# Linear attention and a recurrent block on one Trainium2 core: the last tile's context, the key bias and the last residuals change place

## The chip, the cores and the metric

The kernel runs on one core of a Trainium2 chip. The metric is the device time of one execution in microseconds (us), the median of several. PE is TensorE, DVE is VectorE, ACT is ScalarE, POOL is GpSimd, SP is SyncE (it issues the DMAs here). Each engine executes its own list of instructions in order; what another engine must have done first is a wait on a semaphore that stands in that list, and everything behind a waiting instruction waits too.

## The reference, cut to what matters

The input x is (8, 512, 128) in fp32. A linear attention with a residual and a layer norm is followed by a gated recurrence that scans the first axis, so 8 steps of 512 rows, and a second residual and layer norm.

```python
Q = elu(x @ Wq.T + bq) + 1;  K = elu(x @ Wk.T + bk) + 1;  V = x @ Wv.T + bv
KV = einsum('bnd,bne->bde', K, V)
Z = einsum('bnd,bd->bn', Q, K.sum(axis=1) + 1e-06)
x = layernorm(x + (einsum('bnd,bde->bne', Q, KV) / Z[..., None]) @ Wo.T + bo)
def step(c, xt):                       # over x[0], x[1], ... x[7]
    ft = sigmoid(xt @ wf.T + c @ uf.T + bf);  it = sigmoid(xt @ wi.T + c @ ui.T + bi)
    gt = tanh(xt @ wc.T + c @ uc.T + bc)
    return ft * c + it * gt
h = tanh(x @ wo.T + c_final @ uo.T + bo)
x = layernorm(x + h)
```

## The kernel before, in words

**Tiles.** A tile is one of the 8 slices of x, 512 rows by 128 features, held as four chunks of 128 rows (C = 4, H = 2 is half of them). D is 128. All of it is loaded at the start, tile by tile, once by rows (`x_rows`) and once transposed (`x_cols`).

**Attention of a tile.** PE forms the keys in the bank `ps_k`: four products of x_cols and Wk (L374), each of them fp32 and two instructions in the trace, and then one matmul of `ones_r` with the row of the key bias plus one (L378), all of one accumulation group. ACT takes the exponential (`key_exp`, L664), and DVE combines it with ps_k to elu + 1 (`key_max`, L878, semaphore k_ok). `queries` (L384), `query_exp` (L669, L670) and `query_sum` (L929) do the same for the queries. `keys_x` (L393) multiplies the keys with x, ACT copies that (`xk_copy`, L713), and `key_values` on PE (L403, L404), with the sums of the keys that POOL forms (`key_sums`, L283, L288), gives key-values already multiplied with Wo; DVE adds a constant (`key_values`, L937, semaphore kvo_ok). These small products lie in the bank of `ps_ctx` in the columns behind the context, and for tile 7 in `ps_k` (function `small`, L198). `context` (L415) multiplies the queries with them: 2 x 2 blocks of 129 columns, the last of which is Z, in the two banks of `ps_ctx`. DVE takes 1/Z (`reciprocal_z`, L861), and `residual` (L867) adds x, one chunk at a time; its semaphores y_ok and y_small_ok say that the two banks of the context are free. `attention_end` is residual, `statistics` (L841) and `variance` (L847).

**First layer norm.** POOL raises variance + eps to the power -1/2 (`reciprocal_root`, L292); DVE normalises chunks (L856). For tiles 0, 6 and 7 (SHARED_LN) ACT does two of the four chunks (`first_normalise`, L708), for which POOL first makes a shift (L297). PE turns the tile (`x1_turned`, L429) into `ps_x1`, from which ACT takes a rounded high part (`x1_high`, L717), DVE the rest (`x1_low`, L873) and ACT a whole copy (`x1_whole`, L721).

**Recurrence.** The three gates stand in the banks ps_f, ps_i and ps_c. `gates_x` (L443 to L452) adds the products of x1 in split precision, `gate_s` (L470 to L475) those of the state, high part and low part; they need `state_high` on ACT (L688) and `state_low` on POOL (L316), in two late steps on DVE (L914). `gates_tanh` on ACT (L678) is three tanhs: forget, input, candidate. DVE forms `kept_state` (L889), `new_state` (L896) and `next_state` (L903), together `step`. The list STEPS (L47) orders the steps: 0 to 3 are tiles 0 to 3 in full width; after that each tile is stepped in two halves, the lower halves of tiles 4 to 7 being steps 4, 5, 7 and 8, the upper ones 6, 9, 10 and 11.

**The order.** The first FULL_PERIODS periods (L239) are generated: in period n every engine does its share of the keys and queries of tile n + 1, the key-values and context of tile n, the first layer norm of tile n - 1 and the recurrence of tile n - 2. After them the order of every engine is written out by hand (POOL from L345, PE from L618, ACT from L760, DVE from L983). In it keys_x, key_values and context of tile 7 stand around the gates of step 5 on PE.

**Output.** UNITS (L52) divides the output into nine units of tiles and halves: units 0 to 3 are the lower halves of two tiles each, 4 to 6 the upper halves of two tiles, 7 and 8 the upper halves of tile 6 and of tile 7. Each has a bank (`unit_bank`, L159). PE forms the product with wo (`out_x`, L506), and adds what all tiles share, the final state's product, either directly (`out_s`, L522, units 0 and 4) or from a rounded copy in two parts g_hi and g_lo (`out_g`, `add_g`, L547, L551). ACT takes the tanh in place in the bank (`out_tanh`, L697, h_ok), DVE adds it to x1 (`second_residual`, L1010, w_ok), then `second_statistics` (L1018) and `second_variance` (L1026, L1028). POOL makes the root and the shift (L303, L310). The blocks of a unit are normalised by DVE (the first DVE_NORM[u], L1034) and ACT (the others, L702), and SP stores the unit when both have done (L265). In the last loops DVE does, for units 5 to 8, residual, statistics, variance of the unit and its share of normalise of the unit before; ACT does the tanh of unit u and its share of normalise of unit u - 2.

## Time and profile before

| | us |
|---|---|
| median of 3 runs | 105.56 (105.0 to 105.93) |
| the profiled execution, its own time | 106.08 |
| its span, first to last instruction | 104.3 |
| PE busy | 92.1 (88%) |
| DVE busy | 81.4 (78%) |
| ACT busy | 66.3 (64%) |
| POOL busy | 43.0 (41%) |

The granted clock of TensorE is 0.974 of full speed on the mean. All numbers of the trace are in us from the span's start. A line such as L374 is a line of the kernel before. In rows of a timeline the bracket at the end is how long the engine was idle before the instruction, and what ended that. A busy PE is modelled: matmuls overlap, and the duration shown is longer than the distance to the next one; the chain shows the distance.

### The profile page before, as it was taken

The numbers are of one execution on the slowest core, as the hardware profiler recorded it, in microseconds if no ns is written. First come the engines' busy times: TensorE is split into PE (matmuls) and PEld (weight loads), VectorE is DVE, ScalarE is ACT, GpSimd is POOL, SyncE is SP. The second block draws the span as 40 slices with busy tenths as digits, with TensorE's granted clock in tenths as the row PEclk, the third lists the DMA queues.
The fourth block names the chain that finished last, engine by engine and source line by source line (L and its number), as shares of the span: only waits on it lengthen the run. The fifth ranks groups of instructions, "written<-read, shape, count | busy, mean of one in ns | idle before, by whom it ended". The sixth has DMA issues, their size and how long they took to land.

```text
span 104.3 us, 1923 instructions
## 1 busy us (share of the span) xinstructions
PE 92.1 (88%) x611; PEld 79.7 (76%) x611; DVE 81.4 (78%) x236; ACT 66.3 (64%) x137; POOL 43.0 (41%) x64
## 2 busy tenths in 40 slices
PE   6998999999799999999999999998999999986000
PEld 4778779689388968978888989988899998965000
DVE  3136398979999995898689997986356999999960
ACT  1327579476485594576659565759465859777651
POOL 2006268328448048019206622650500238266660
PEclk9999999999999999999999999999999999999955
DMA  2869996000000000000000000000000000443362
GB/s 40 287 214 409 384 387 236 0 0 3 0 0 0 0 0 0 9 0 0 0 0 0 0 6 0 0 3 3 6 0 0 0 0 6 158 137 108 105 209 89
DMA packets 5269, 7.30 MB, mean 70 GB/s; under 512 B 491, under 2 KB 3084, under 8 KB 5260
## 3 DMA queue, kind: packets, MB, share of 16 engines
q1 hardware_dynamic: 4828, 6.85, 18.7%
q10 hardware_dynamic: 432, 0.33, 1.2%
q8 instruction: 5, 0.08, 0.4%
q14 instruction: 4, 0.03, 0.1%
HBM read 5.08 MB, written 2.10 MB: 69 GB/s over the span
## 4 chain that ended last, share of the span: by engine, by line
PE 54%; DVE 32%; issue 4%; ACT 4%; POOL 2%; POOLq 0%; DVEq 0%; ACTq 0%
PE ps_k L374 7%; PE ps_ctx L393 6%; DVE stats L1018 6%; PE ps_q L384 6%; DVE x L1010 5%; PE ps_ctx L415 4%; PE ps_f L363 4%; DVE x L856 4%; DVE s L903 2%; DVE x L1034 2%; DVE new L896 2%; PE ps_x L429 2%; PE ps_f L452 2%; PE ps_k L378 2%; PE ps_ctx L403 2%
## 5 line engine op out<-in xcount | busy, mean ns | idle before, releaser
L316 POOL TENSOR_TENSOR s_lo<-s,s_hi 128x512 fp32r<-128x512 f32 (+1 forms) x8 | 8.1, 1016 | 22.7 <-ACT s_hi L688 22.7
L303 POOL TENSOR_TENSOR rstd<-var_eps,minus_half 128x4 f32<-128x4 f32 (+1 forms) x9 | 9.3, 1034 | 13.8 <-DVE var_eps L1026 13.8
L292 POOL TENSOR_TENSOR rstd<-var_eps,minus_half 128x4 f32<-128x4 f32 x8 | 9.0, 1122 | 9.3 <-DVE var_eps L847 9.0
L702 ACT ACTIVATE x<-x,shift,rstd 128x128 f32<-128x128 f32 x20 | 8.6, 488 | 3.0 <-POOL shift L310 2.8
L283 POOL TENSOR_TENSOR k_pair<-k_rows 128x256 f32<-128x256 f32 x8 | 6.3, 784 | 9.8 <-DVE k_rows L878 9.8
L856 DVE TENSOR_SCALAR x<-x,stats,rstd 128x128 f32<-128x128 f32 x26 | 9.9, 439 | 0.3 <-POOL rstd L292 0.3
L664 ACT ACTIVATE k_exp<-ps_k,minus_one 128x512 f32<-128x512 f32 x8 | 5.5, 686 | 6.2 <-PE ps_k L378 6.2
L374 PE MATMUL ps_k<-wkq,x_cols 128*128 128x128 f32 x64 | 9.3, 294 | 0.0
L867 DVE SCALAR_TENSOR_TENSOR x<-ps_ctx,z_inv,x_rows 128x128 f32<-128x128 f32 x32 | 9.1, 343 | 0.1
L374 PEld LDWEIGHTS ps_k<-wkq,x_cols 128*128 128x128 f32 x64 | 8.6, 209 | 0.4 <-DMA wkq<-w_kq 0.4
L717 ACT ACTIVATE x_hi<-ps_x 128x512 fp32r<-128x512 f32 x8 | 4.8, 597 | 6.5 <-PE ps_x L429 6.5
L415 PEld LDWEIGHTS ps_ctx<-kvo,q_cols 128*128 128x128 f32 x64 | 8.2, 191 | 0.8 <-issue 0.5
L678 ACT ACTIVATE th_f<-ps_f,half_b 128x256 f32<-128x256 f32 (+1 forms) x11 | 5.8, 529 | 4.7 <-PE ps_f L475 4.4
L415 PE MATMUL ps_ctx<-kvo,q_cols 128*128 128x129 f32 x64 | 8.5, 276 | 0.0
L384 PE MATMUL ps_q<-x_cols,wkq 128*128 128x512 f32 x16 | 8.2, 592 | 0.0
L393 PEld LDWEIGHTS ps_ctx<-k_rows,x_rows 128*128 128x128 f32 x56 | 7.1, 191 | 1.0 <-issue 0.7
L393 PE MATMUL ps_ctx<-k_rows,x_rows 128*128 128x128 f32 x56 | 7.5, 277 | 0.4 <-DVE k_rows L878 0.4
L688 ACT ACTIVATE s_hi<-s 128x256 fp32r<-128x256 f32 (+1 forms) x10 | 4.9, 499 | 4.2 <-DVE s L903 4.2
L889 DVE SCALAR_TENSOR_TENSOR keep<-th_f,s 128x256 f32<-128x256 f32 (+1 forms) x11 | 5.4, 491 | 2.7 <-ACT th_f L678 2.7
L896 DVE SCALAR_TENSOR_TENSOR new<-th_i,th_c 128x256 f32<-128x256 f32 (+1 forms) x12 | 6.1, 509 | 1.7 <-ACT th_c L678 1.7
L678 ACT ACTIVATE th_i<-ps_i,half_b 128x256 f32<-128x256 f32 (+1 forms) x11 | 5.8, 527 | 2.0 <-PE ps_i L475 2.0
L903 DVE SCALAR_TENSOR_TENSOR s<-keep,new 128x256 f32<-128x256 f32 (+1 forms) x12 | 6.2, 515 | 0.8
(176 smaller groups left out, 283.3 us busy)
## 6 DMA issues: line engine op xcount, KB each, us to landing
x_cols<-xt SPq DMA_DIRECT2D x8, 256.0 KB, 7.0
x_rows<-x SPq DMA_DIRECT2D x8, 256.0 KB, 7.0
out<-x SPq DMA_DIRECT2D x7, 256.0 KB, 2.2
wgate<-w_gate SPq DMA_DIRECT2D x1, 384.0 KB, 6.9
out<-x SPq DMA_DIRECT2D x2, 128.0 KB, 1.8
wkq<-w_kq ACTq DMA_DIRECT2D x1, 131.0 KB, 3.7
wvo_in<-w_vo_in ACTq DMA_DIRECT2D x1, 128.0 KB, 3.7
wout<-w_out SPq DMA_DIRECT2D x1, 128.0 KB, 6.5
```

Of the source, the lines that this page charges most:

```text
L292: nc.gpsimd.tensor_tensor(rstd[:, b], var_eps[:, b], minus_half[:], ALU.pow).then_inc(rstd_ok, 1)
L303: nc.gpsimd.tensor_tensor(part_of(rstd, u, T), part_of(var_eps, u, T), minus_half[:, 0:nt * H].rearrange("p (t c) -> p t c", c=H), ALU.pow ...
L374: nc.tensor.matmul(ps_k[:, c * D:(c + 1) * D], x_cols[:, a, c], wkq[:, WK_T * D:(WK_T + 1) * D], start=(c == 0), stop=False, skip_group_ch ...
L384: nc.tensor.matmul(ps_q[:], wkq[:, WQ_T * D:(WQ_T + 1) * D], x_cols[:, a].rearrange("p c d -> p (c d)"), start=True, stop=True).then_inc(q ...
L393: mm = nc.tensor.matmul(small(a)[:, 0:D], x_rows[:, a, c], k_rows[:, a % 2, c], start=(c == 0), stop=(c == C - 1))
L415: mm = nc.tensor.matmul(ctx_view[:, c // 2, c % 2], q_cols[:, b % 2, c], kvo[:, b % 2], start=True, stop=True, skip_group_check=True)
L678: nc.scalar.activation(out_tile[:, part], ps[:, part], ACT.Tanh, bias=bias, scale=scale).then_inc(ok, 1)
L702: nc.scalar.activation(x1[:, t, c], x1[:, t, c], ACT.Identity, bias=shift[:, t, c:c + 1], scale=rstd[:, T + t, c:c + 1]).then_inc(y2_act_o ...
L856: nc.vector.tensor_scalar(x1[:, b, c], x1[:, b, c], mean_of(b, c), rstd[:, b, c:c + 1], ALU.subtract, ALU.mult).then_inc(x1_ok, 1)
L867: ins = nc.vector.scalar_tensor_tensor(x1[:, b, c], ctx_view[:, c // 2, c % 2, 0:D], z_inv[:, b % 2, c:c + 1], x_rows[:, b, c, 0:D], ALU.m ...
L896: nc.vector.scalar_tensor_tensor(new[:, part], th_i[:, part], 1.0, th_c[:, part], ALU.add, ALU.mult).then_inc(new_ok, 1)
L903: nc.vector.scalar_tensor_tensor(state(t)[:, part], keep[:, part], 0.5, new[:, part], ALU.mult, ALU.add).then_inc(s_ok, 1)
```

## The change

1. *Key bias.* For tiles 4 to 7 ACT writes the key bias plus one into `ps_k` (a new function `key_bias`, placed between the forget tanh and the input tanh of the period before), and the four key products accumulate on it, so that the bias matmul is not issued. The bias is loaded once more, to all 128 partitions (64 KB, SP's queue, behind wgate), and POOL adds one to it after `halve_weights`.
2. *Tile 7.* The generated periods are six; the seventh is written out together with what followed. In it keys_x, key_values and context of tile 7 follow those of tile 6, before the gates of step 5. The context of tile 7 lies in banks of its own, ps_k (behind the small products) and ps_q, so that it waits for no residual of tile 6. DVE does the residual of tile 7 ahead of step 5 and its statistics behind it; ACT and POOL follow that order. On ACT the xk copy of tile 7 stands between the forget tanh and the input tanh of step 4. The banks of the units change accordingly: units 0 and 1 take those of ps_ctx, units 2 and 3 ps_k and ps_q.
3. *Last units.* For units 6, 7 and 8 PE adds x1 onto the tanh in PSUM, with the identity as the stationary operand (`add_x1`); DVE's residual is left out, and the statistics and the normalise read the sum from PSUM. DVE_NORM of units 5 to 8 goes from 1, 2, 1, 1 to 2, 0, 2, 2.

The diff, cut to its core:

```diff
          (7, 0, H), (5, H, C), (6, H, C), (7, H, C)]
-FULL_PERIODS = 7
+FULL_PERIODS = 6
 UNITS = [(0, 2, 0), (2, 2, 0), (4, 2, 0), (6, 2, 0), (0, 2, H), (2, 2, H), (4, 2, H), (6, 1, H), (7, 1, H)]
-DVE_NORM = [1, 1, 1, 2, 2, 1, 2, 1, 1]
+DVE_NORM = [1, 1, 1, 2, 2, 2, 0, 2, 2]
+IN_PSUM = (6, 7, 8)
 SHARED_LN = (0, 6, 7)
+BIAS_BY_PE = 4
...
         ctx_view = ps_ctx[:, :, 0:2 * DZ].rearrange("p b (c d) -> p b c d", d=DZ)
-        g_bank = [ps_x1[:, 0:H * D], ps_q[:, 0:H * D]]
-        unit_bank = [ps_k[:], ps_q[:], ps_ctx[:, 0, :], ps_ctx[:, 1, :], ps_x1[:], ps_k[:], ps_ctx[:, 0, :],
-                     ps_ctx[:, 1, :], ps_f[:]]
+        g_bank = [ps_x1[:, 0:H * D], ps_ctx[:, 1, 0:H * D]]
+        unit_bank = [ps_ctx[:, 0, :], ps_ctx[:, 1, :], ps_k[:], ps_q[:], ps_x1[:], ps_ctx[:, 0, :], ps_k[:], ps_q[:],
+                     ps_f[:]]
         kq_in, vo_in, gate_in, out_in = sem("kq_in"), sem("vo_in"), sem("gate_in"), sem("out_in")
-        row_in, batt_in = sem("row_in"), sem("batt_in")
+        row_in, batt_in, bk_in = sem("row_in"), sem("batt_in"), sem("bk_in")
...
                     sp.dma_start(wgate[:], w_gate).then_inc(gate_in, 16)
+                    sp.dma_start(bk_wide[:], rows[BK_ROW].partition_broadcast(D)).then_inc(bk_in, 16)
...
                                         ALU.mult).then_inc(shift1_ok, 1)
+            def key_bias():
+                pool.wait_ge(bk_in, 16)
+                nc.gpsimd.tensor_scalar(bk_wide[:], bk_wide[:], 1.0, None, ALU.add).then_inc(bk_ok, 1)
...
                     halve_weights()
+                    key_bias()
...
                     split_state_low()
+            state_low(3)
+            reciprocal_root(5)
+            key_sums(7)
...
                     pe.wait_ge(k_ok, a)
+                if a >= BIAS_BY_PE:
+                    pe.wait_ge(k_bias_ok, a - BIAS_BY_PE + 1)
                 for c in range(C):
-                    nc.tensor.matmul(ps_k[:, c * D:(c + 1) * D], x_cols[:, a, c], wkq[:, WK_T * D:(WK_T + 1) * D],
-                                     start=(c == 0), stop=False, skip_group_check=True)
+                    mm = nc.tensor.matmul(ps_k[:, c * D:(c + 1) * D], x_cols[:, a, c], wkq[:, WK_T * D:(WK_T + 1) * D],
+                                          start=(c == 0 and a < BIAS_BY_PE), stop=(a >= BIAS_BY_PE),
+                                          skip_group_check=True)
+                if a >= BIAS_BY_PE:
+                    mm.then_inc(k_mm, 1)
+                    return
...
                 pe.wait_ge(kvo_ok, b + 1)
-                if b >= 1:
+                if 1 <= b < T - 1:
                     pe.wait_ge(y_ok, b)
-                if b == T - 1:
-                    pe.wait_ge(y_small_ok, b)
                 for c in range(C):
-                    mm = nc.tensor.matmul(ctx_view[:, c // 2, c % 2], q_cols[:, b % 2, c], kvo[:, b % 2],
+                    mm = nc.tensor.matmul(ctx_of(b, c // 2)[:, c % 2], q_cols[:, b % 2, c], kvo[:, b % 2],
...
                     pe.wait_ge(out_in, 16)
-                    pe.wait_ge(kvo_ok, T)
+                    pe.wait_ge(y_ok, T - 1)
                 if u == 1:
-                    pe.wait_ge(q_relu_ok, T)
+                    pe.wait_ge(y_small_ok, T - 1)
...
                                  start=False, stop=True, skip_group_check=True).then_inc(out_mm, 1)
+            def add_x1(u):
+                t0, nt, c0 = UNITS[u]
+                ps = unit_bank[u]
+                pe.wait_ge(h_ok, u + 1)
+                for j in range(nt):
+                    mm = nc.tensor.matmul(ps[:, j * H * D:(j + 1) * H * D], ident[:],
+                                          x1[:, t0 + j, c0:c0 + H].rearrange("p c d -> p (c d)"),
+                                          start=False, stop=True, skip_group_check=True)
+                mm.then_inc(psum_w_mm, 1)
...
                     x1_turned(b)
+            keys(7)
+            queries(7)
+            gates_x(4)
+            keys_x(6)
+            gate_s(0, 4)
+            key_values(6)
             keys_x(7)
+            gate_s(1, 4)
+            gate_s(2, 4)
+            context(6)
+            key_values(7)
+            x1_turned(5)
+            context(7)
             gates_x(5)
-            key_values(7)
             gates_s(5)
-            context(7)
...
                 add_g(u)
+                if u - 1 in IN_PSUM:
+                    add_x1(u - 1)
+            add_x1(len(UNITS) - 1)
...
                 nc.scalar.activation(out_tile[:, part], ps[:, part], ACT.Tanh, bias=bias, scale=scale).then_inc(ok, 1)
-            def gates_tanh(k):
+            def forget_tanh(k):
                 tanh(ps_f, f_mm, k, keep_ok, th_f, 0.5, half_b[:, 0:1] if k else first_b[:, 0:1], f_ok)
+            def input_tanh(k):
...
                 tanh(ps_c, c_mm, k, new_ok, th_c, 1.0, col[:, BC:BC + 1] if k else first_b[:, 2:3], c_ok)
+            def gates_tanh(k):
+                forget_tanh(k)
+                input_tanh(k)
...
                 for t, c in blocks(u)[DVE_NORM[u]:]:
-                    nc.scalar.activation(x1[:, t, c], x1[:, t, c], ACT.Identity, bias=shift[:, t, c:c + 1],
-                                         scale=rstd[:, T + t, c:c + 1]).then_inc(y2_act_ok, 1)
+                    nc.scalar.activation(x1[:, t, c], sum_of(u)[:, t - UNITS[u][0], c - UNITS[u][2]], ACT.Identity,
+                                         bias=shift[:, t, c:c + 1], scale=rstd[:, T + t, c:c + 1]).then_inc(y2_act_ok, 1)
...
                                          scale=rstd[:, b, c:c + 1]).then_inc(x1_act_ok, 1)
+            def key_bias(a):
+                if a == BIAS_BY_PE:
+                    act.wait_ge(bk_ok, 1)
+                act.wait_ge(k_ok, a)
+                nc.scalar.activation(ps_k[:].rearrange("p (c d) -> p c d", d=D),
+                                     bk_wide[:].unsqueeze(1).to_broadcast([D, C, D]), ACT.Copy).then_inc(k_bias_ok, 1)
...
                 if t is not None:
-                    gates_tanh(t)
+                    forget_tanh(t)
+                    key_bias(k + 1)
+                    input_tanh(t)
...
                     x1_high(b)
+            key_exp(7)
+            state_high(3)
+            x1_whole(4)
+            query_exp(7)
+            xk_copy(6)
+            forget_tanh(4)
+            xk_copy(7)
+            input_tanh(4)
+            x1_high(5)
             state_high(4)
-            xk_copy(7)
...
             gates_tanh(5)
+            first_normalise(6)
             state_high(5)
-            first_normalise(6)
+            x1_high(6)
             gates_tanh(6)
-            x1_high(6)
...
                 dve.wait_ge(ctx_mm, b + 1)
-                nc.vector.reciprocal(z_inv[:, b % 2].rearrange("p (b c) -> p b c", c=2),
-                                     ctx_view[:, :, :, D]).then_inc(z_ok, 1)
+                if b < T - 1:
+                    nc.vector.reciprocal(z_inv[:, b % 2].rearrange("p (b c) -> p b c", c=2),
+                                         ctx_view[:, :, :, D]).then_inc(z_ok, 1)
+                    return
+                for half in range(2):
+                    nc.vector.reciprocal(z_inv[:, b % 2, half * H:half * H + H], ctx_of(b, half)[:, :, D]).then_inc(z_ok, 1)
             def residual(b, chunks, done):
-                dve.wait_ge(z_ok, b + 1)
+                dve.wait_ge(z_ok, b + 1 if b < T - 1 else T + 1)
                 for c in chunks:
-                    ins = nc.vector.scalar_tensor_tensor(x1[:, b, c], ctx_view[:, c // 2, c % 2, 0:D],
+                    ins = nc.vector.scalar_tensor_tensor(x1[:, b, c], ctx_of(b, c // 2)[:, c % 2, 0:D],
...
                     next_state(t)
-                if b >= 1 and a < FULL_PERIODS - 1:
+                if b >= 1:
                     x1_low(b)
+            attention_end(5)
+            key_max(7)
+            query_sum(7)
+            key_values(6)
+            normalise(5)
+            kept_state(4)
+            new_state(4)
+            reciprocal_z(6)
+            key_values(7)
+            next_state(4)
...
             dve.wait_ge(y_small_ok, 7)
-            key_values(7)
...
             variance(6)
+            reciprocal_z(7)
+            residual(7, range(H, C), y_small_ok)
+            residual(7, range(H), y_ok)
+            normalise(6)
             step(5)
-            normalise(6)
-            reciprocal_z(7)
-            attention_end(7)
-            kept_state(6)
+            dve.wait_ge(y_ok, 8)
+            dve.wait_ge(y_small_ok, 8)
+            statistics(7)
+            variance(7)
             x1_low(6)
+            step(6)
             normalise(7)
-            new_state(6)
-            next_state(6)
...
                 t0, nt, c0 = UNITS[u]
-                dve.wait_ge(w_ok, u + 1)
+                if u in IN_PSUM:
+                    dve.wait_ge(psum_w_mm, IN_PSUM.index(u) + 1)
+                else:
+                    dve.wait_ge(w_ok, u + 1)
...
                     st = nc.vector.bn_stats(stats[:, T + t, c0:c0 + H].rearrange("p c m -> p (c m)"),
-                                            x1[:, t, c0:c0 + H].rearrange("p c d -> p d c"))
+                                            sum_of(u)[:, t - t0].rearrange("p c d -> p d c"))
...
                 for t, c in blocks(u)[:DVE_NORM[u]]:
-                    nc.vector.tensor_scalar(x1[:, t, c], x1[:, t, c], mean_of(T + t, c), rstd[:, T + t, c:c + 1],
-                                            ALU.subtract, ALU.mult).then_inc(y2_ok, 1)
+                    nc.vector.tensor_scalar(x1[:, t, c], sum_of(u)[:, t - UNITS[u][0], c - UNITS[u][2]], mean_of(T + t, c),
+                                            rstd[:, T + t, c:c + 1], ALU.subtract, ALU.mult).then_inc(y2_ok, 1)
...
             for u in range(5, len(UNITS)):
-                second_residual(u)
+                if u not in IN_PSUM:
+                    second_residual(u)
...
```

In the part that is cut, `sum_of(u)` is the bank of the unit for units 6 to 8 and x1 for the others, and `ctx_of(b, half)` is ps_ctx for tiles 0 to 6, and for tile 7 `ps_k[:, DZ:3*DZ]` (half 0) and `ps_q[:, 0:2*DZ]` (half 1).

## Rows read from the trace of the kernel before

**Rows 1.** The page's first part: busy time, share, instructions.
```profile
PE 92.1 (88%) x611; PEld 79.7 (76%) x611; DVE 81.4 (78%) x236; ACT 66.3 (64%) x137; POOL 43.0 (41%) x64
```
**Rows 2.** Stages: length, PE, PEld, DVE, ACT, POOL busy; clock, DMA share, GB/s.
```profile
30.00:40.00 10.00, 10.00 (x63) 8.50 (x62) 9.85 (x27) 7.13 (x13) 5.24 (x6) 1.00 0.00 0
70.00:80.00 10.00, 9.64 (x76) 9.06 (x76) 5.75 (x14) 6.39 (x17) 1.72 (x3) 1.00 0.01 2
```
**Rows 3.** The chain that ended last, tile 6's keys: start, us, what.
```profile
44.21 0.89 PE ps_k L374 x8
45.10 0.23 PE ps_k L378
```
**Rows 4.** The same chain between units 5 and 7.
```profile
95.82 0.60 DVE x L1010
...
97.48 0.25 DVE x L1034
97.73 0.34 DVE x L1010
```
**Rows 5.** Timeline of PE at 27 us and of DVE at 50 us.
```profile
26.91 0.59 PE L429 MATMUL ps_x<-ident,x 128*128 128x128 f32 x2 [0.56 <-DVE x L856]
...
50.36 0.29 DVE L937 TENSOR_TENSOR kvo<-ps_ctx,eps_z 128x129 f32<-128x129 f32 x1 [1.19 <-PE ps_ctx L404]
```
**Rows 6.** Timeline of ACT, period of tiles 5 and 6.
```profile
45.96 0.62 ACT L688 ACTIVATE s_hi<-s 128x512 fp32r<-128x512 f32 x1
...
51.05 0.69 ACT L678 ACTIVATE th_i<-ps_i,half_b 128x512 f32<-128x512 f32 x1 [0.45 <-PE ps_i L475]
```
**Rows 7.** Timeline of POOL; then a DMA issue, the last number its landing.
```profile
15.54 1.48 POOL L292 TENSOR_TENSOR rstd<-var_eps,minus_half 128x4 f32<-128x4 f32 x1 [0.73 <-DVE var_eps L847]
...
26.73 0.54 POOL L330 TENSOR_SCALAR uo_half<-wout 128x128 f32<-128x128 f32 x1
...
wgate<-w_gate SPq DMA_DIRECT2D x1, 384.0 KB, 6.9
```
**Rows 8.** Timeline of ACT and PE around steps 4 and 8.
```profile
58.52 0.47 ACT L678 ACTIVATE th_i<-ps_i,half_b 128x256 f32<-128x256 f32 x1 [0.67 <-PE ps_i L475]
...
71.23 0.60 PE L429 MATMUL ps_x<-ident,x 128*128 128x128 f32 x4
```
**Rows 9.** Timeline of DVE, states 4 and 5, tile 7's norm; POOL's root of tile 7.
```profile
60.51 0.42 DVE L903 SCALAR_TENSOR_TENSOR s<-keep,new 128x256 f32<-128x256 f32 x1
...
65.41 0.42 DVE L903 SCALAR_TENSOR_TENSOR s<-keep,new 128x256 f32<-128x256 f32 x1
...
66.53 1.13 DVE L867 SCALAR_TENSOR_TENSOR x<-ps_ctx,z_inv,x_rows 128x128 f32<-128x128 f32 x4
67.69 0.77 DVE L841 BATCH_NORM_STATS2 stats<-x 128x6 f32<-128x256 f32 x2
...
73.33 0.69 DVE L873 TENSOR_TENSOR x_lo<-ps_x,x_hi 128x512 fp32r<-128x512 f32 x1
...
68.74 1.18 POOL L292 TENSOR_TENSOR rstd<-var_eps,minus_half 128x4 f32<-128x4 f32 x1 [1.64 <-DVE var_eps L847]
```
**Rows 10.** Timeline of ACT and POOL in the last ten us.
```profile
94.14 0.58 ACT L697 ACTIVATE ps_ctx<-ps_ctx 128x512 f32<-128x512 f32 x1
...
96.81 1.26 ACT L702 ACTIVATE x<-x,shift,rstd 128x128 f32<-128x128 f32 x3 [1.02 <-POOL shift L310]
...
101.64 0.49 ACT L702 ACTIVATE x<-x,shift,rstd 128x128 f32<-128x128 f32 x1 [1.17 <-POOL shift L310]
...
100.38 0.79 POOL L303 TENSOR_TENSOR rstd<-var_eps,minus_half 128x2 f32<-128x2 f32 x1 [0.43 <-DVE var_eps L1026]
```
**Rows 11.** Groups by line and form: busy us, mean ns of one.
```profile
L867 DVE SCALAR_TENSOR_TENSOR x<-ps_ctx,z_inv,x_rows 128x128 f32<-128x128 f32 x32 | 9.1, 343 | 0.1
...
L1018 DVE BATCH_NORM_STATS2 stats<-x 128x6 f32<-128x256 f32 x16 | 6.2, 424 | 0.2
...
L1034 DVE TENSOR_SCALAR x<-x,stats,rstd 128x128 f32<-128x128 f32 x12 | 3.8, 341 | 0.6 <-POOL rstd L303 0.6
```

More of the change, by code:

```diff
@@ L97, in build @@
         batt = sb("batt", [D, D])
+        bk_wide = sb("bk_wide", [D, D])
         ident = sb("ident", [D, D])
@@ L200, in small, with ctx_of @@
             return ps_k[:, 0:DZ] if a == T - 1 else ps_ctx[:, 1, 2 * DZ:3 * DZ]
+        def ctx_of(b, half):
+            if b < T - 1:
+                return ctx_view[:, half]
+            tile = ps_q[:, 0:2 * DZ] if half else ps_k[:, DZ:3 * DZ]
+            return tile.rearrange("p (c d) -> p c d", d=DZ)
         def dve_chunks(b):
@@ L243, in periods, with sum_of @@
                 yield n + 1, n, n - 1 if n >= 1 else None, n - 2 if n >= 2 else None
+        def sum_of(u):
+            nt = UNITS[u][1]
+            if u in IN_PSUM:
+                return unit_bank[u][:, 0:nt * H * D].rearrange("p (t c d) -> p t c d", c=H, d=D)
+            return part_of(x1, u)
         def act_norms(units):
```

4 lines of the change are left out of this document (added).

## The prediction, made before the changed kernel was run

> **What bounds the kernel now.** I read the page's shares first, then the stages, then the chain that ended last, then the engines one by one where the change acts. The shares name PE (92.1 us of 104.3) with DVE behind it (81.4) [rows 1]. An average hides the order, so the stages come next: from 30 to 40 us PE is busy for all of 10 us, from 70 to 80 us DVE for only 5.75 [rows 2]. So there are three regimes. In the periods the chain is PE alone, a tile's four key products (0.89 us) and the key bias (0.23) back to back [rows 3]. From 58 to 80 us the chain goes to and fro between layer norms and the recurrence. From 80 us it is DVE without a gap: residual, statistics, variance, normalise, unit after unit [rows 4].
>
> **Key bias by ScalarE.** Four bias matmuls (tiles 4 to 7) leave PE, 4 x 0.235 = 0.94 us [rows 3]. Tile 4's is worth nothing: right behind it PE waits 0.56 us for DVE's normalise of tile 1, which neither edit touches [rows 5]. The other three lie in the unbroken PE chain: 0.70 us. That holds if DVE and ACT keep up. DVE idles 1.19 us per period before the kvo addition, so a period shorter by 0.23 leaves it slack [rows 5]. ACT gets a 128x512 write per period; the nearest row is the copy s_hi of that shape, 0.62 us [rows 6]. It stands between the forget and the input tanh, where ACT idles 0.45 us waiting for PE [rows 6]. So the input tanh moves by about 0.1 us and the candidate tanh, which waits for PE itself, by nothing. Bounds: 0 if another engine takes over, 0.94 if tile 4's counts too; I take 0.70. The extra DMA (64 KB, issued after wgate) and POOL's addition of 1.0 (a 128x128 POOL tensor_scalar took 0.54 us) fit the gap on POOL before the first root, 0.73 us [rows 7]. If the DMA landed late, POOL's queue would hold the root of tile 0; wgate, the issue before it, took 6.9 us to land, and the addition would run from 14.8, the start of that gap [rows 7]. I cost it at 0, at most 0.5.
>
> **Tile 7's context one period up.** No work disappears; its order changes on four engines. I walked both orders by hand with the durations of the trace, entering 0.70 us early. What is queued behind each wait decides:
> - ACT now holds the input and candidate tanh of step 4 behind the xk copy of tile 7. Before, th_i(4) ran at 58.52 [rows 8]. Now key_values(6) frees PE at about 57.4, keys_x(7) (0.89) is read at 58.5, the copy (0.28) ends at 58.75, th_i starts at 58.85 and th_c ends at 59.7. On DVE next_state(4) also stands behind the kvo addition of tile 7, whose matmuls follow context(6): 60.5. State 4 starts at 60.75; before it was 60.51 [rows 9].
> - The first half of what follows keeps its lead: statistics(6) start at about 62.8. Residual(7) goes out at 64.05 against 66.53, 2.5 us sooner [rows 9].
> - But residual(7) (1.13 us), its two reciprocals (0.2) and normalise(6) (0.5) now stand ahead of step 5. State 5 starts at 66.5 against 65.41: 1.1 us later [rows 9]. Statistics(7) stand behind step 5: 66.9 against 67.69. POOL does s_lo(5) up to 68.2 and only then root(7), 1.18 us by its row, and its shift; ACT's share of normalise(7) starts at 69.85 and PE turns the tile at 70.75 against 71.23 [rows 8, 9]. x_lo(7) follows at 72.85 against 73.33 [rows 9].
> So of the 0.70 us about 0.5 arrives at the steps 8 to 11. From there to 93 us both kernels issue the same instructions with the same waits, on other banks whose last users are done by then; the 0.5 us goes through unchanged. The bounds of this part: +1.2 (the lead kept, and layer norm 7 no longer behind s_lo(5) on POOL, 0.5) and -1.1 (state 5's delay carried through). I take +0.5.
>
> **x1 added in PSUM.** DVE loses the residual of units 6, 7, 8: 0.60 + 0.34 + 0.34 = 1.28 us [rows 4]. Its share of normalise goes from 1, 2, 1, 1 to 2, 0, 2, 2 blocks for units 5 to 8, plus 0.26. In return each unit goes tanh, PE, DVE. By the row of four 128-column f32 products (0.89 us for 512 columns [rows 3]) the identity product costs 0.87 us for unit 6 and 0.43 for units 7 and 8. In the times of before: tanh(6) ends 94.72 [rows 10], the product is readable at 95.9, where DVE is free at 95.8 after normalise(4): 0.1 lost. Statistics(6) to 96.65, variance, normalise(5) with 2 blocks to 97.4; unit 7's sum was ready at 97.05, so statistics(7) run at 97.4. Unit 8 is late: ACT's normalise(5) waits for shift(5) and starts at 96.81 [rows 10], now 2 blocks to 97.6, tanh(8) to 97.95, product to 98.65, statistics to 99.1, variance to 99.3, by the chain of before (0.43 for one unit of 256 columns [rows 11]). POOL: root(6) 96.9 to 98.0, root(7) to 99.1, root(8) 99.35 to 100.15 (0.79 by its row [rows 10]). DVE normalises both blocks of unit 8 up to 100.8. Before, the chain ended with shift(8) and an ACT block at 101.64 + 0.49 = 102.13 [rows 10]. That is 1.3 us. The store of unit 8 now stands behind those of 6 and 7 in SP's queue and in the transfers: 0.1 back. Net 1.2.
> Not shown before are statistics, DVE and ACT normalises that read PSUM. DVE's residual, which reads a 128x128 block from PSUM, took 343 ns, the normalise from SBUF 341, statistics 424 [rows 11]: so 0 to 0.06 us for each of six instructions on the path, 0.1 taken, and ACT's four blocks are off the path.
> The Trainium skill speaks against this edit: "VectorE: DVE Perf Modes", section "Why PSUM operands drop a tier", says that an operand in PSUM caps fp32 at the single rate, where tensor_scalar from SBUF can have the double. By it the normalises of units 7 and 8 would take some 0.07 us more each, an estimate of 0.2 us on the path. The rows of SBUF and PSUM above are 2 ns apart, so the trace does not yet show the double rate being lost.
>
> **The sum.** Span 104.3 - 0.5 - 1.2 = 102.6. The profiled run took 106.08, 1.78 more than its span: 104.4. It stands 0.52 above the median of 105.56; taking that off gives **103.9 us**, 1.6% less. About 1% is what a measurement of this kernel tells from no change.
>
> **Rivals.**
> 1. *Only the tail gains (20%).* The restructured stretch eats the 0.70: th_i(4) 1.0 us behind its old place relative to the rest, and state 5 late, speak for it; that layer norm 7, not state 5, opened step 8 before, speaks against. 104.3 - 1.2 = 103.1 span, 104.4 on the median's scale.
> 2. *The tail is lost to hand-overs (12%).* The middle gives its 0.5, but tanh to PE to DVE costs as much as the residuals saved: if each of the three sums came 0.4 us after DVE is free, 1.2 us is gone. Against it: only unit 8's is late in my walk. 105.1.
> 3. *The middle gains more (13%).* DVE is idle for 4.25 of the 10 us from 70 to 80 [rows 2]; if the residual, 2.5 us sooner, lets layer norm 7 open step 8 by the whole lead of 0.70 and the 0.5 in which POOL holds its root, the exit lead is 1.2 and the time 103.2.
> 4. *Slower (7%).* The recurrence becomes the bound at step 5. The delays placed ahead of it add in full: tanh 0.94, reciprocals and residual(7) 1.33, normalise(6) 0.5, together 2.8; less 0.70 at entry it is 2.1 late, less 1.2 in the tail: 0.9 above before, 106.5. It decides once state 5 is written after about 68 us; my walk has 66.9, and steps 6 and 9, which do not need it, give cover.
> 5. *It does not do what it says (3%).* The bias by ACT comes after PE has reached the next keys, so that PE waits: tile 4's is ready at about 24.75 against 24.83, but there 0.56 us of slack follows; the later ones are written some 2 us before PE's next keys. With a wait of 0.4 us at each of three tiles it is 1.2 above the forecast, 105.1.
>
> **How the numbers follow.** My forecast has 45%, with its own range 103.3 to 104.5. Rivals 1, 3, 2, 5 and 4 reach from 103.2 to 106.5; leaving out 4 and part of 2, 5 and 3 gives 102.8 to 105.2. Faster by over 1% (below 104.5): the forecast nearly whole (0.43), rival 3 (0.13) and somewhat over half of rival 1 (0.12): 0.68. Slower by over 1% (above 106.6): half of rival 4 and what I overlooked, 0.07. The rest, 0.25, is within 1%.
>
> **What would show it.** Right: period length on PE 8.6 us instead of 8.83; ACT's bias write 0.6 us; state 5 later than before by about a microsecond while PE turns tile 7 about 0.5 earlier; no DVE residual for units 6 to 8, DVE waiting only for unit 8; the chain ending in POOL's root and a DVE normalise. Wrong: DVE waiting for PE at every one of the last three units; PE idle for over 1 us in all between 58 and 72 us; step 8's forget tanh starting later than 75.2 less 0.3.

## The result, and the profile after

The changed kernel took 103.94 us in the median of four executions (103.33 to 104.32), the kernel before 105.28 in the same comparison: ratio 0.9857, 95% interval 0.9815 to 0.9899. A later comparison of the same two gave 0.9843 (0.9799 to 0.9887). The forecast was 103.9 us. The profiled execution took 104.32 us with a span of 102.4, against 106.08 and 104.3. So the device time holds 1.92 us that lie outside the span, against 1.78 before.

The page's first part, of the changed kernel:
```profile
PE 93.8 (92%) x615; PEld 80.7 (79%) x615; DVE 80.6 (79%) x235; ACT 67.5 (66%) x140; POOL 42.7 (42%) x65
```
Its stages, columns as in [rows 2]:
```profile
30.00:40.00 10.00, 10.00 (x64) 8.56 (x63) 9.85 (x27) 7.56 (x14) 5.22 (x6) 1.00 0.00 0
70.00:80.00 10.00, 9.87 (x79) 9.31 (x78) 5.28 (x14) 6.52 (x17) 1.42 (x2) 1.00 0.01 2
```
The shares tell little: PE has more busy time than before (rows of matmuls overlap, and one that waits is drawn longer), and the gain lies in the order of work. What tells is the time between landmarks. I use five: the start of ACT's high part of tile 1 (A, 27.53 us before), PE's query product of tile 7 (B), the forget tanh of step 8 (C), DVE's statistics of unit 5 (D), the end of the last compute instruction (E), and the span's end (F).

| us | start to A | A to B | B to C | C to D | D to E | E to F |
|---|---|---|---|---|---|---|
| before | 27.53 | 26.48 | 21.15 | 19.11 | 7.86 | 2.17 |
| changed | 27.52 | 25.78 | 20.95 | 19.08 | 6.71 | 2.36 |
| difference | -0.01 | -0.70 | -0.20 | -0.03 | -1.15 | +0.19 |

The sum is 1.9 us. Three of the six stretches carry it. In the chain of the changed kernel (start, us, what) tile 6's keys and queries now touch, where [rows 3] had the bias between them:
```profile
43.95 0.89 PE ps_k L408 x8
44.85 0.86 PE ps_q L422 x2
```
PE's period is 8.61 us here (44.85 to 53.46), as forecast. ACT's write of the bias (L781) stands between the two tanhs. In [rows 6], two periods later, ACT waited 0.45 us at that place, as in the two periods before it. In the changed kernel the input tanh follows without a wait. The input and the candidate tanh start 1.13 and 1.83 us behind the forget tanh, against 1.14 and 1.84 before, so the write costs them nothing. Tile 4's write is the exception: ACT had no wait there, and the input tanh came 0.77 us later (24.71 against 23.94), without effect on A. The write of tile 5:
```profile
32.23 0.69 ACT L737 ACTIVATE th_f<-ps_f,half_b 128x512 f32<-128x512 f32 x1 [0.42 <-PE ps_f L511]
32.81 0.59 ACT L781 ACTIVATE ps_k<-bk_wide 128x512 f32<-128x512 f32 x1
33.36 0.69 ACT L737 ACTIVATE th_i<-ps_i,half_b 128x512 f32<-128x512 f32 x1
34.06 0.69 ACT L737 ACTIVATE th_c<-ps_c,wkq 128x512 f32<-128x512 f32 x1
```
For tile 4 PE's wait for DVE grew from 0.56 to 0.63 us, as [rows 5] let expect, so that matmul's removal brought nothing. POOL's addition filled the gap of [rows 7]; the root still starts where it did:
```profile
26.90 0.59 PE L465 MATMUL ps_x<-ident,x 128*128 128x128 f32 x2 [0.63 <-DVE x L939]
...
14.76 0.55 POOL L326 TENSOR_SCALAR bk_wide<-bk_wide 128x128 f32<-128x128 f32 x1
15.53 1.48 POOL L315 TENSOR_TENSOR rstd<-var_eps,minus_half 128x4 f32<-128x4 f32 x1 [0.22 <-DVE var_eps L930]
```
The stretch around tile 7, on DVE, which answers to [rows 9]:
```profile
60.59 0.41 DVE L990 SCALAR_TENSOR_TENSOR s<-keep,new 128x256 f32<-128x256 f32 x1
...
63.91 0.61 DVE L954 SCALAR_TENSOR_TENSOR x<-ps_q,z_inv,x_rows 128x128 f32<-128x128 f32 x2
...
66.32 0.42 DVE L990 SCALAR_TENSOR_TENSOR s<-keep,new 128x256 f32<-128x256 f32 x1
66.67 0.76 DVE L924 BATCH_NORM_STATS2 stats<-x 128x6 f32<-128x256 f32 x2
67.46 0.57 DVE L930 TENSOR_SCALAR var_eps<-stats 128x4 f32<-128x4 f32 x1
...
72.42 0.68 DVE L960 TENSOR_TENSOR x_lo<-ps_x,x_hi 128x512 fp32r<-128x512 f32 x1
```
State 4 is written 0.08 us later than before and state 5 0.91 us later, while the statistics of tile 7 come 1.0 sooner and its low part 0.91 sooner. PE's turn of the tile, in the next rows, comes 0.64 sooner (70.59 against 71.23). POOL's subtraction and root, ACT's share of tile 7's norm and PE's turn of it:
```profile
67.28 0.73 POOL L344 TENSOR_TENSOR s_lo<-s,s_hi 128x256 fp32r<-128x256 f32 x1 [2.17 <-ACT s_hi L753]
68.11 1.01 POOL L315 TENSOR_TENSOR rstd<-var_eps,minus_half 128x4 f32<-128x4 f32 x1
...
69.49 0.88 ACT L773 ACTIVATE x<-x,shift,rstd 128x128 f32<-128x128 f32 x2 [0.16 <-POOL shift L320]
...
70.59 0.60 PE L465 MATMUL ps_x<-ident,x 128*128 128x128 f32 x4
```
The tail, on DVE. No residual stands between unit 5's and unit 8's blocks any more. DVE waits 0.70 us for PE at unit 8. At unit 6 it loses 0.2: the statistics start 0.72 us behind a pair of normalise blocks, where 0.51 is the usual distance (95.94 to 96.45):
```profile
95.00 0.76 DVE L1119 BATCH_NORM_STATS2 stats<-ps_k 128x6 f32<-128x256 f32 x2
95.79 0.17 DVE L1127 TENSOR_SCALAR var_eps<-stats 128x4 f32<-128x4 f32 x1
95.87 0.16 DVE L1129 TENSOR_SCALAR minus_mean<-stats 128x4 f32<-128x4 f32 x1
95.94 0.60 DVE L1135 TENSOR_SCALAR x<-x,stats,rstd 128x128 f32<-128x128 f32 x2
96.45 0.42 DVE L1119 BATCH_NORM_STATS2 stats<-ps_q 128x6 f32<-128x256 f32 x1
...
97.87 0.43 DVE L1119 BATCH_NORM_STATS2 stats<-ps_f 128x6 f32<-128x256 f32 x1 [0.70 <-PE ps_f L597]
...
99.31 0.73 DVE L1135 TENSOR_SCALAR x<-ps_f,stats,rstd 128x128 f32<-128x128 f32 x2
```

### The profile page after: what moved, and what is told of

It is laid out like the page before. It is cut to its first block, busy times and chain, and to the rows that moved or that the text cites. A ratio compares the mean times of both kernels' runs of the same rounds, so it can differ in the third digit from the quotient of the medians.

```text
span 102.4 us, 1942 instructions
## 1 busy us (share of the span) xinstructions
PE 93.8 (92%) x615; PEld 80.7 (79%) x615; DVE 80.6 (79%) x235; ACT 67.5 (66%) x140; POOL 42.7 (42%) x65
## 4 chain that ended last, share of the span: by engine, by line
PE 57%; DVE 27%; issue 5%; ACT 4%; POOL 3%; DVEq 0%; POOLq 0%; ACTq 0%
PE ps_k L408 7%; PE ps_ctx L431 6%; PE ps_q L422 6%; PE ps_ctx L451 5%; DVE stats L1119 5%; PE ps_f L395 4%; DVE x L1108 4%; DVE x L939 3%; PE ps_x L465 2%; DVE s L990 2%; DVE x L954 2%; DVE new L983 2%; POOL rstd L331 2%; PE ps_ctx L441 2%; DVE x L1135 2%
## 5 line engine op out<-in xcount | busy, mean ns | idle before, releaser
L954 DVE SCALAR_TENSOR_TENSOR x<-ps_ctx,z_inv,x_rows 128x128 f32<-128x128 f32 x28 | 8.0, 342 | 0.1
L451 PEld LDWEIGHTS ps_ctx<-kvo,q_cols 128*128 128x128 f32 x56 | 7.2, 191 | 0.8 <-issue 0.5
L451 PE MATMUL ps_ctx<-kvo,q_cols 128*128 128x129 f32 x56 | 7.5, 276 | 0.0
L767 ACT ACTIVATE x<-x,shift,rstd 128x128 f32<-128x128 f32 x15 | 6.4, 486 | 1.0 <-POOL shift L338 1.0
L965 DVE SCALAR_TENSOR_TENSOR k_rows<-k_exp,ps_k 128x512 f32<-128x512 f32 x8 | 5.4, 680 | 1.9 <-ACT k_exp L723 1.9
```

The costliest lines, as they stand in the source:

```text
L451: mm = nc.tensor.matmul(ctx_of(b, c // 2)[:, c % 2], q_cols[:, b % 2, c], kvo[:, b % 2], start=True, stop=True, skip_group_check=True)
L767: nc.scalar.activation(x1[:, t, c], sum_of(u)[:, t - UNITS[u][0], c - UNITS[u][2]], ACT.Identity, bias=shift[:, t, c:c + 1], scale=rstd[:, ...
L954: ins = nc.vector.scalar_tensor_tensor(x1[:, b, c], ctx_of(b, c // 2)[:, c % 2, 0:D], z_inv[:, b % 2, c:c + 1], x_rows[:, b, c, 0:D], ALU. ...
```

## The experiments

Each was profiled and timed beside the kernel before. The time from start to A differs from one execution to the next (26.5 to 27.5 us, taken up at the end), so spans are not compared directly; stretches are. The table gives them; the timed ratios have intervals of +-0.25 to 0.45%, and decide less. The time outside the span is not the same for all kernels either: in the medians it is 1.80 us before, 1.80 in tile7_only, 1.77 in psum_only, 1.94 in bias_psum, 1.92 in the changed kernel, 2.12 in bias_only and 2.12 in two_queues. No stretch shows it, and why it differs stays open.

| us | start to A | A to B | B to C | C to D | D to E | E to F | ratio, 95% interval |
|---|---|---|---|---|---|---|---|
| bias_only | 26.89 | 25.78 | 21.23 | 19.12 | 7.86 | 2.22 | 0.9968 (0.9943 to 0.9992) |
| tile7_only | 26.62 | 26.49 | 20.97 | 19.11 | 7.85 | 2.16 | 0.9982 (0.9954 to 1.0010) |
| psum_only | 26.77 | 26.48 | 21.11 | 19.10 | 6.72 | 2.32 | 0.9909 (0.9877 to 0.9942) |
| bias_psum | 26.92 | 25.79 | 21.23 | 19.09 | 6.72 | 2.35 | 0.9876 (0.9844 to 0.9908) |
| changed_again | 27.52 | 25.78 | 20.98 | 19.11 | 6.70 | 2.41 | 0.9843 (0.9799 to 0.9887) |
| step4_back | 26.96 | 25.79 | 20.98 | 19.10 | 6.73 | 2.34 | 0.9831 (0.9793 to 0.9869) |
| step5_first | 26.51 | 25.80 | 21.46 | 19.12 | 6.72 | 2.39 | 0.9821 (0.9790 to 0.9853) |
| slo5_dve | 27.35 | 25.79 | 20.88 | 19.12 | 6.71 | 2.35 | 0.9814 (0.9775 to 0.9854) |
| tanh8_first | 26.76 | 25.78 | 20.96 | 19.11 | 6.55 | 2.54 | 0.9833 (0.9790 to 0.9877) |
| tanh8_noshift | 26.78 | 25.79 | 20.96 | 19.11 | 6.24 | 2.82 | 0.9842 (0.9801 to 0.9884) |
| both_parts | 27.46 | 25.79 | 20.88 | 19.09 | 6.24 | 2.84 | 0.9847 (0.9807 to 0.9887) |
| two_queues | 27.04 | 25.79 | 20.96 | 19.11 | 6.27 | 2.23 | 0.9839 (0.9801 to 0.9877) |

### Each part alone

**bias_only.** The bias edit of the change's diff, on the kernel before, with its seven periods.

> The kernel before with only the key bias of tiles 4 to 7 written by ScalarE. Theory (PE sets the periods, three of the four matmuls lie in its chain): the query product of tile 7 starts 0.70 us sooner than 54.01, and the forget tanh of step 8 as well, since nothing between re-orders: 74.5 against 75.16; span 103.6, ratio 0.993. Rival A (the lead is eaten by the DVE and POOL chain from 58 us on): step 8 within 0.2 us of before, ratio 1.0. Rival B (tile 4's matmul counts too): 0.94.

The 0.70 us appears at B to the hundredth, so tile 4's matmul is worth nothing. At C 0.62 is left; a tenth is eaten on the way. The timed ratio, 0.9968, is smaller than the 0.993 expected, whose value lies just outside the interval; the stretches after A sum to 0.56 us less, 0.995. The spans of all executions agree with the stretches: their median is 103.1 us against 103.7. About half of that is lost again outside the span, 2.12 us against 1.80.

**tile7_only.** The changed kernel with
```diff
-BIAS_BY_PE = 4
+BIAS_BY_PE = 8
-DVE_NORM = [1, 1, 1, 2, 2, 2, 0, 2, 2]
+DVE_NORM = [1, 1, 1, 2, 2, 1, 2, 1, 1]
-IN_PSUM = (6, 7, 8)
+IN_PSUM = ()
```
and without the calls of key_bias and of the last add_x1, and the bias's DMA.

> The changed kernel with the key bias back on PE for all tiles and the x1 sums of units 6 to 8 back on DVE (old split of the normalise), so only tile 7's order and banks differ from before. Theory of the prediction (re-ordering costs 0.2 us): step 8's forget tanh at 75.4 against 75.16, ratio 1.002. Rival, from the changed kernel's trace (lead 0.71 at tile 7's keys, 0.91 at step 8): the re-ordering gains 0.2 us of its own: 74.95, ratio 0.998. Second rival: it gains only together with the bias, so here it is 0.

B to C is 0.18 us shorter than before: the first rival. The re-ordering gains by itself, where I had forecast a loss of 0.2. The next part shows from what.

**psum_only.** The PSUM edit on the kernel before (banks and order as before).

> The kernel before with only x1 of units 6 to 8 added by PE in PSUM and the changed split of the normalise; banks as before. Theory: last DVE normalise ends about 1.15 us sooner than the last instruction of before (102.13), some 0.2 us comes back in the stores: span 103.3, ratio 0.991. Rival (tail and middle interact, the tail's gain needs the earlier middle): ratio above 0.996.

D to E falls by 1.14 us and E to F rises by 0.15; nothing else moves. The tail's gain does not depend on the middle.

**bias_psum.** Both, without tile 7's re-ordering.

> Everything of the change but tile 7's order and banks. If parts add: 0.7 + 0.95 = 1.65 us less than before, span 102.65, ratio 0.984, and the whole change differs from this by the worth of tile 7's re-ordering alone, +0.2 by the prediction (the whole change slower) or -0.2 by the trace. Rival: without the re-ordering the 0.7 does not reach the end, ratio 0.991.

A to F is 75.18 us here, 76.77 before and 74.88 in the changed kernel: parts of 1.6 and 0.3 us. Tile 7's order is worth 0.25 to 0.28 us between B and C, somewhat more than alone (0.18). The difference between 0.9876 and 0.9843 has the right sign but is inside the intervals.

### What carries the middle

The way from A to C can be cut at two places of tile 7's layer norm, the start of POOL's root and the start of ACT's share of the normalise:

| us | A to POOL's root | root to ACT's normalise | ACT's normalise to C |
|---|---|---|---|
| before | 41.21 | 1.65 | 4.77 |
| bias_only | 40.60 | 1.65 | 4.76 |
| tile7_only | 41.31 | 1.38 | 4.77 |
| bias_psum | 40.61 | 1.65 | 4.76 |
| changed | 40.59 | 1.38 | 4.76 |
| step5_first | 41.11 | 1.39 | 4.76 |
| slo5_dve | 40.22 | 1.69 | 4.76 |

The last column is fixed. In ACT's list the three tanhs of step 7 stand right behind that normalise, state 7 needs them, and on DVE x_lo(7) stands behind state 7. So PE's earlier turn of the tile does not pass its lead on:
```profile
70.28 0.45 ACT L737 ACTIVATE th_f<-ps_f,half_b 128x256 f32<-128x256 f32 x1
...
72.08 0.42 DVE L990 SCALAR_TENSOR_TENSOR s<-keep,new 128x256 f32<-128x256 f32 x1
```
The re-ordering by itself (tile7_only against before) brings the statistics of tile 7 0.29 us sooner. The variance behind them takes 0.57 instead of 0.17, so the root starts 0.10 later. Root and shift then take 0.27 less. All of the gain lies in these two small instructions of POOL, and the edit was not made for it. Beside the bias the root starts as early as without the re-ordering (40.59 against 40.61), and the whole 0.27 is kept.

**step4_back.**
```diff
             key_values(6)
-            keys_x(7)
             gate_s(1, 4)
             gate_s(2, 4)
+            keys_x(7)
             context(6)
...
             forget_tanh(4)
-            xk_copy(7)
             input_tanh(4)
+            xk_copy(7)
...
+            next_state(4)
             reciprocal_z(6)
             key_values(7)
-            next_state(4)
```

> The changed kernel with the gates of step 4 ahead of tile 7's keys_x on PE, the input tanh of step 4 ahead of tile 7's xk copy on ScalarE, and state 4 ahead of tile 7's kvo addition on VectorE. Theory (state 4's delay lies under the turn of tile 5 and costs nothing): state 4 starts near 59.9 instead of 60.59, step 8's forget tanh within 0.15 us of 74.25. Rival (the recurrence is what carries the middle): all of it 0.5 to 0.7 sooner, span 101.8.

State 4 started at 59.37, with a start to A shorter by 0.56: 59.93 on the changed kernel's scale, 0.66 sooner. B to C stayed (20.98 against 20.95). State 4's delay costs nothing.

**step5_first.**
```diff
-            reciprocal_z(7)
-            residual(7, range(H, C), y_small_ok)
-            residual(7, range(H), y_ok)
-            normalise(6)
             step(5)
+            normalise(6)
+            reciprocal_z(7)
+            residual(7, range(H, C), y_small_ok)
+            residual(7, range(H), y_ok)
```

> The changed kernel with step 5 and normalise of tile 6 ahead of the reciprocals and residual of tile 7 on VectorE. Theory (layer norm 7 opens step 8, state 5 has slack): state 5 starts 1.0 us sooner, statistics of tile 7 about 0.4 later than 66.67, and step 8's forget tanh 0.3 to 0.5 later than 74.25; span 102.8. Rival (recurrence bound): step 8 0.5 to 1.0 sooner.

DVE's timeline of that run:
```profile
64.29 0.43 DVE L990 SCALAR_TENSOR_TENSOR s<-keep,new 128x256 f32<-128x256 f32 x1
...
66.57 0.77 DVE L924 BATCH_NORM_STATS2 stats<-x 128x6 f32<-128x256 f32 x2
```
With 1.01 us added for the earlier A, state 5 is at 65.30 (1.0 sooner than 66.32) and the statistics at 67.58 (0.9 later, more than the 0.4 expected). Step 8's tanh came 0.51 later: of the 0.91 us, 0.40 came back, because the variance of tile 7 no longer runs beside POOL's subtraction and takes 0.17 instead of 0.57. An earlier state at the price of a later layer norm loses: layer norm 7 opens step 8, by the route through ACT's list above. That rules out the mechanism of my rival 4.

**slo5_dve.** The first hunk is POOL's list, the second DVE's.
```diff
             first_shift(6)
-            state_low(5)
             reciprocal_root(7)
...
             variance(7)
+            state_low(5)
             x1_low(6)
```

> The changed kernel with the low part of state 5 taken from POOL to VectorE, behind variance(7). In the changed kernel's trace that variance took 0.57 us, ending as POOL's subtraction ends, and root(7) started at 68.11. Theory (POOL's subtraction holds both): variance(7) takes 0.17, root(7) starts near 67.7, step 8's forget tanh 0.3 to 0.4 sooner than 74.25. Rival (PE's gates of step 7 decide when the tile is turned): variance faster, but step 8 unchanged, or 0.3 later by the 0.34 us more on VectorE.

```profile
67.32 0.17 DVE L929 TENSOR_SCALAR var_eps<-stats 128x4 f32<-128x4 f32 x1
...
67.47 0.42 DVE L1000 TENSOR_TENSOR s_lo<-s,s_hi 128x256 fp32r<-128x256 f32 x1
67.57 1.18 POOL L315 TENSOR_TENSOR rstd<-var_eps,minus_half 128x4 f32<-128x4 f32 x1 [2.61 <-DVE var_eps L929]
68.90 0.33 POOL L320 TENSOR_TENSOR shift<-minus_mean,rstd 128x2 f32<-128x2 f32 x1
```
The first half held: the variance took 0.17 instead of 0.57, the root started 0.37 sooner (67.74 after adding 0.17 for the earlier A, against 68.11). The second half fell: root and shift took 1.18 and 0.33 instead of 1.01 and 0.20, and B to C gained only 0.07. What differs in the rows is the instruction that DVE is in when the root starts: here s_lo, in the changed kernel x_lo, and in the kernel before `keep` of step 6. The last two, first the changed kernel, then the one before:
```profile
68.02 0.68 DVE L960 TENSOR_TENSOR x_lo<-ps_x,x_hi 128x512 fp32r<-128x512 f32 x1
...
68.64 0.42 DVE L889 SCALAR_TENSOR_TENSOR keep<-th_f,s 128x256 f32<-128x256 f32 x1
```
In all fourteen traces tile 7's root takes 1.18 us where DVE is in `keep` or s_lo, both of whose inputs are in SBUF (six traces), and 1.01 where it is in x_lo, one of whose inputs is in PSUM (eight). That these go together is shown; that the one causes the other was not tested apart.

### What ends the tail

**tanh8_first.**
```diff
                 out_tanh(7)
-                normalise(5)
                 out_tanh(8)
+                normalise(5)
```

> The changed kernel with ScalarE's tanh of unit 8 ahead of its share of normalise of unit 5. Theory (behind the tanh, POOL's queue of roots and shifts holds root(8) at 98.58 anyway): statistics of unit 8 0.6 to 0.7 us sooner than 97.87, root(8) within 0.15 us of 98.58, span unchanged at 102.4. Rival (the chain shown, normalise, tanh, sum, statistics, is the bound): 0.6 us less, span 101.8.

The statistics of unit 8 began 3.84 us after D instead of 4.54, root(8) 5.09 instead of 5.25. D to F is 9.09 against 9.07. The theory held: the chain as printed ran through ACT's normalise and tanh, but POOL's queue was next within 0.16 us. The end of the span did not follow even that, which the next run takes up. (The span itself was 101.7, all of it by the shorter start to A.)

**tanh8_noshift.**
```diff
                 second_root(u)
-                second_shift(u)
+                if u < 7:
+                    second_shift(u)
```

> The kernel with unit 8's tanh first, and POOL leaves out the shifts of units 7 and 8, which no block uses since VectorE normalises both whole. Theory: root(8) follows root(7) at once, 98.2 instead of 98.58, last normalise 0.3 to 0.4 us sooner than in the changed kernel, span 102.0. Rival as before: if the tanh alone had already brought 0.6, this adds nothing.

The edit stands on top of tanh8_first. E came 0.47 us sooner, more than asked, and F not at all: D to F is 9.06. The new bound is the stores. SP issues them in order, here in the changed kernel units 6 and 8, and in this run unit 8:
```profile
99.10 0.37 SPq L288 DMA_DIRECT2D out<-x  x1
...
100.08 0.40 SPq L288 DMA_DIRECT2D out<-x  x1
```
```profile
99.39 0.40 SPq L288 DMA_DIRECT2D out<-x  x1
```
In both, the three issues lie 5.77, 6.24 and 6.75 us after D. Unit 6 goes first, as soon as ACT has ended its four blocks, 5.70 us after D in both, and the other two follow 0.47 and 0.51 us apart. In the changed kernel unit 8 was ready at 6.71, so its store did not wait; here it is ready at 6.24 and waits half a us. From the last issue to the span's end it is 2.3 us in both, and 2.1 in the kernel before. DMA share by stage, first this kernel, then the changed one (the three last columns: granted clock, share, GB/s). The clock falls to 0.50, the level of 1.2 GHz, only after PE's last product, which ends at 97.76 in the changed kernel, so it costs nothing:
```profile
99.50:100.00 0.50, 0.00 (x0) 0.00 (x0) 0.00 (x0) 0.00 (x0) 0.00 (x0) 1.00 1.03 344
100.00:100.50 0.50, 0.00 (x0) 0.00 (x0) 0.00 (x0) 0.00 (x0) 0.00 (x0) 1.00 1.05 342
```
```profile
100.00:100.50 0.50, 0.00 (x0) 0.00 (x0) 0.04 (x1) 0.00 (x0) 0.00 (x0) 0.50 0.96 324
100.50:101.00 0.50, 0.00 (x0) 0.00 (x0) 0.00 (x0) 0.00 (x0) 0.00 (x0) 0.50 1.04 344
101.00:101.50 0.50, 0.00 (x0) 0.00 (x0) 0.00 (x0) 0.00 (x0) 0.00 (x0) 0.50 1.02 338
```
Units 6, 7 and 8 become ready within 0.7 us, SP issues them half a us apart, and 512 KB move at about 340 GB/s in one block.

**both_parts.** This one and slo5_dve together.

> Unit 8's tanh first, no shifts for units 7 and 8, and the low part of state 5 on VectorE, together. If both theories hold, 0.3 to 0.4 in the middle and 0.35 in the tail: span 101.7 and a ratio to before of 0.978, against 0.986 for the changed kernel.

It has both small effects, 20.88 and 6.24, and still D to F of 9.08. The forecast of 0.978 was missed, 0.9847; neither of the effects it was built on reaches the end.

**changed_again.**

> The changed kernel unaltered, for comparison on the same chip with the three others and with the four runs of single parts: ratio 0.986 as at first, span 102.4. Against the version without tile 7's re-ordering (0.9876) it tells what that is worth in time: 0.2 us by the traces.

The stretches repeat to 0.05 us, the ratio to 0.0014.

**two_queues.** On top of tanh8_noshift, unit 6 is stored in two, the first half by SP (first hunk), the second from ACT's list (second hunk):
```diff
+                nt = 1 if u == 6 else nt
                 sp.wait_ge(y2_ok, sum(DVE_NORM[:u + 1]))
-                sp.wait_ge(y2_act_ok, act_norms(u + 1))
+                sp.wait_ge(y2_act_ok, act_norms(6) + 2 if u == 6 else act_norms(min(u + 1, 6)))
...
             normalise(6)
+            act.wait_ge(y2_act_ok, act_norms(7))
+            act.dma_start(out[5:6].rearrange("t (p c) d -> p t c d", c=C)[:, :, H:C],
+                          x1[:, 5:6, H:C]).then_inc(stored, 16)
```

> The run with unit 8's tanh first and without two shifts, and the store of unit 6 in two: its first tile by SP as soon as ScalarE has normalised it, its second by ScalarE's own queue. In the run before this edit the last compute ended 6.24 us after the statistics of unit 5 began (6.71 in the changed kernel), but the span ended 9.06 us after them, as in the changed kernel (9.07): SP issued the stores of units 6, 7 and 8 half a us apart, and the transfers ran from 99.3 to 100.9 at 340 GB/s. Theory (the three stores, issued and moved one behind the other, end the span): the first tile moves 0.7 us sooner, the last store is issued 0.4 sooner, the span ends 8.5 to 8.7 us after the statistics of unit 5; ratio to before 0.980. Rival (what follows the last issue is a fixed latency of some 2.3 us that no ordering shortens, and the last issue does not move): 9.0.

SP's first half of unit 6 and units 7 and 8, and ACT's second half:
```profile
98.01 0.34 SPq L289 DMA_DIRECT2D out<-x  x1
...
98.53 0.34 SPq L289 DMA_DIRECT2D out<-x  x1
99.20 0.33 SPq L289 DMA_DIRECT2D out<-x  x1
...
98.67 0.35 ACTq L885 DMA_DIRECT2D out<-x  x1
```
D to F is 8.50 us, 0.57 less than in the changed kernel. The last issue now follows E directly, 6.30 us after D instead of 6.75: that is 0.45 of the 0.57, and 0.12 is saved behind it. So it was SP's list, with unit 6 at its head, that ended the span, and the transfer of all three in one block only to a small part. With it loosened the two edits on ACT and POOL pay: in the changed kernel unit 8 was ready only at 6.71, so the split store alone could hardly have brought anything (an estimate from these rows; no run has it alone). In time the gain could not be told apart: 0.9839 against 0.9843, where the stretches let expect 0.979. Of the difference 0.2 us is time outside the span, 2.12 us against 1.92. It is the shortest by its profile, not shown to be by the time.

**unit6_split.** On top of tanh8_noshift DVE was to take one of unit 6's four blocks, to relieve ACT; D to F was expected at 8.65 us. It has no time: DVE and ACT would read the bank of that unit at once, with nothing ordering them. What it would gain stays open.

## Why the prediction was right, step by step

- *Key bias, -0.70.* Right to the hundredth at B; 0.61 of it arrives at tile 7's root. The cover was the one named: tile 4's in PE's wait for DVE, ACT's write in its wait for PE, but for tile 4's. The write took 596 ns on the mean; 0.62 had been taken.
- *Tile 7, forecast -0.2 of gain, measured +0.18 alone and +0.25 to 0.28 beside the bias.* This term had the wrong sign. The mechanism of the walk was right: state 5 late by 0.91 (1.1 forecast), harmless; layer norm 7 decides, as step5_first shows. What failed is the size of its steps, one above all. The walk let the root start at 68.2 (68.11 measured) and ACT's normalise at 69.85 (69.49). The distance between them, 1.65 us, is that of the kernel before, with a root of 1.18 us; measured were 1.38, with a root of 1.01. So of the 0.36 us by which the walk is late there, 0.27 is POOL's root and shift, taken from a row beside which DVE did something else, and 0.09 is rounding up to that point. The walk also handed on the lead of PE's turn, 0.48 forecast and 0.64 measured; what reaches step 8 is the lead of ACT's normalise, 0.90. So 0.9 us instead of 0.5 reached step 8. By these rows the re-ordering without the shorter root would have been worth about nothing beside the bias, and a loss of 0.1 alone.
- *Tail, -1.2, measured -1.15 + 0.19 = -0.96.* The compute part was 1.3 forecast, 1.15 measured; the stores gave back 0.19, not 0.1, because from the last issue to the span's end it is 2.3 us instead of 2.1. Unit 8 was late, as walked: DVE waited 0.70 us there, and 0.2 at unit 6, where 0.1 had been walked. In us from D, the tanh of unit 8 ended at 3.68 as walked, its statistics started at 4.54 (4.38 walked), the last normalise at 5.98 (5.88). The forecast had put this wait down to ACT's normalise(5); tanh8_first shows that POOL's roots were level with it.
- *Reads from PSUM, 0.1 us.* Groups by form, mean ns of one:
```profile
L1135 DVE TENSOR_SCALAR x<-x,stats,rstd 128x128 f32<-128x128 f32 x9 | 2.7, 342 | 0.0
...
L1135 DVE TENSOR_SCALAR x<-ps_f,stats,rstd 128x128 f32<-128x128 f32 x2 | 0.7, 404 | 0.1
...
L1119 DVE BATCH_NORM_STATS2 stats<-x 128x6 f32<-128x256 f32 x12 | 4.6, 422 | 0.1
L1119 DVE BATCH_NORM_STATS2 stats<-ps_k 128x6 f32<-128x256 f32 x2 | 0.8, 422 | 0.1
```
  The normalise from PSUM takes 62 ns more, the statistics nothing. The Trainium skill, "VectorE: DVE Perf Modes", section "Why PSUM operands drop a tier", had it right for the normalise: I had estimated 0.07 us by it, and set beside that the residual's row, an instruction with two tensor inputs, which was the wrong neighbour. The two blocks of unit 8 took 0.73 us, against 0.65 in the walk and 0.60 from SBUF: 0.08 us of the tail's shortfall is this.
- *The total.* 1.9 us by the stretches against 1.7 forecast; the error of +0.4 in the middle and of -0.25 in the tail partly cancelled. Also, the forecast counted down from a median of 105.56 us and left the time outside the span as it was; it grew by 0.14. Against the 105.28 us measured beside it, the gain was 1.34 us, 1.4%, and 1.62 in the repetition, where 1.66 had been forecast. That the median agreed within 0.1 us is luck in part, and better than the steps deserved.
- *Rivals.* Only the tail gains: B to C shows 0.2 us on top of the 0.70. The tail lost to hand-overs: one wait of 0.70 us and one of 0.2, and 0.96 kept. The middle gains more: half of the way, 0.9 where 0.5 was forecast and 1.2 was the rival's, but through the shorter root and not through POOL's subtraction, behind which layer norm 7 still stood. Slower: state 5 was written at 66.7, under the 68 named, and had slack.

## What to carry to other kernels

When a chain passes through several engines, walk it with the distance from one start to the next in the trace rather than with durations and rounded gaps. When an edit changes what DVE does beside a POOL instruction, the old row of that instruction is no longer its price: here that was worth 0.27 us, more than the re-ordering itself. For an operand in another memory, take the neighbour row with the same kind of operands. When the last units of work become faster, look at when their stores are issued: they become ready together, one list issues them half a us apart, and the one at its head can hold all the others. Compare stretches between landmarks, which repeat to 0.05 us here, before believing a total.
